# Context rows of a fused cross-attention issued from GpSimd's queue instead of SyncE's

## The reference, cut to what matters

```python
# x: (16, 64, 256), ctx_1024: (16, 1601, 256)
q = layernorm(x) @ Wq + bq
k = ctx_1024 @ Wk + bk
v = ctx_1024 @ Wv + bv
attn = softmax(einsum('bqd,bkd->bqk', q, k) / 16)
x = x + einsum('bqk,bkd->bqd', attn, v)
# then: selective-scan layer, ffn, windowed attention, masked attention, experts
```

## Time and profile before

| | us |
|---|---|
| median of 3 runs | 666.3 (665.47 to 666.42) |
| the profiled execution | 663.98 |
| its span (first to last instruction) | 662.2 |
| cross-attention, span 0 to about 158 | 158 |
| mean clock granted to TensorE, share of full | 0.994 |

### The profile page before, as it was taken

How to read it: one execution, slowest core, us unless ns; L and a number is a source line. 1 busy time by engine, 2 the same in 40 slices (tenths; PEclk the granted TensorE clock), 3 DMA queues, 4 the chain that set the end, 5 groups by cost and what they waited for, 6 DMA issues and landing times. The chain is left out here.

```text
span 662.2 us, 11724 instructions
## 1 busy us (share of the span) xinstructions
PE 603.9 (91%) x4436; PEld 461.4 (70%) x4436; DVE 465.1 (70%) x795; ACT 368.9 (56%) x700; POOL 235.2 (36%) x190
## 2 busy tenths in 40 slices
PE   8899999989998878878878999999999899999997
PEld 6555544455356767667767788887777767889897
DVE  2663333345867999999999527788978777886554
ACT  2411111124988999999999434334657466556343
POOL 2000000000069999999989200035651021231000
PEclk9899999999999999999999999999999989999999
DMA  8999999993922223232320000000100022210000
GB/s 306 402 402 394 388 393 392 389 334 143 269 75 97 97 97 97 96 127 97 125 97 4 1 1 17 1 0 19 36 2 2 1 65 81 64 49 1 32 1 33
DMA packets 31839, 86.48 MB, mean 131 GB/s; under 512 B 8108, under 2 KB 19848, under 8 KB 29608
## 3 DMA queue, kind: packets, MB, share of 16 engines
q1 hardware_dynamic: 31640, 85.67, 36.4%
q10 hardware_dynamic: 144, 0.06, 0.0%
HBM read 83.50 MB, written 1.11 MB: 128 GB/s over the span
## 5 line engine op out<-in xcount | busy, mean ns | idle before, releaser
L841 POOL TENSOR_TENSOR dbu<-du,bs 128x1024 f32<-128x1024 f32 x64 | 149.9, 2371 | 6.6 <-DVE w_in L1089 4.6
L970 ACT ACTIVATE weighed<-T,CT 128x256 f32<-128x256 f32 x222 | 95.0, 593 | 1.3 <-PE T L1168 0.9
L1089 DVE TENSOR_TENSOR_SCAN w_in<-hS,dbu 128x1024 f32<-128x1024 f32 x42 | 94.6, 2272 | 0.4 <-ACT hS L959 0.4
L959 ACT ACTIVATE hS<-delta,negA 128x504 f32<-128x504 f32 x128 | 90.9, 815 | 4.9 <-DVE xn L1089 2.2
L1182 PE MATMUL Y<-ident,weighed 128*128 128x128 f32 x512 | 66.7, 273 | 0.0
L1168 PE MATMUL T<-ident,w_in 128*128 128x128 f32 x336 | 46.0, 279 | 19.8 <-ACT weighed L970 14.3
L1182 PEld LDWEIGHTS Y<-ident,weighed 128*128 128x128 f32 x512 | 57.9, 141 | 0.5
L1168 PEld LDWEIGHTS T<-ident,w_in 128*128 128x128 f32 x336 | 36.1, 140 | 30.7 <-DVE w_in L1089 27.4
L309 PE MATMUL O<-cN,pT 128*64 128x256 f32 x384 | 46.7, 385 | 6.9 <-DMA cN<-in_ctx 6.9
L421 POOL COPY w_xp<-w_xp 128x64 f32<-128x64 f32 x3 | 0.6, 236 | 144.8 <-DMA w_out<-in_w_out 144.8
L1089 DVE TENSOR_TENSOR_SCAN xn<-hS,dbu 128x1024 f32<-128x1024 f32 x22 | 50.0, 2275 | 2.3 <-ACT hS L959 2.3
(11 more groups left out here) (442 smaller groups left out, 1338.4 us busy)
## 6 DMA issues: line engine op xcount, KB each, us to landing
cN<-in_ctx SPq DMA_DIRECT2D x8, 3072.0 KB, 25.7
cT<-in_ctxT SPq DMA_DIRECT2D x7, 3202.0 KB, 24.7
bs<-b_rows SPq DMA_DIRECT2D x32, 512.0 KB, 3.6
raw_w<-in_w SPq DMA_DIRECT2D x16, 256.0 KB, 2.8
cT<-in_ctxT SPq DMA_DIRECT2D x1, 2048.0 KB, 10.4
w<-in_w SPq DMA_DIRECT2D x7, 256.0 KB, 7.4
cT<-in_ctxT SPq DMA_DIRECT2D x1, 1154.0 KB, 13.5
vs<-vx SPq DMA_DIRECT2D x8, 136.0 KB, 2.3
```

What stands on the lines that cost most here:

```text
L841: e.tensor_tensor(dbu[s % NB][:, :, :], half(m.du, s // DS), row, ALU.mult).then_inc(s_bu, 1)
L959: i = e.activation(by_batch(A[s % 2][:, j * HALF:(j + 1) * HALF]), by_batch(m.delta[:, c, h * HALF:(h + 1) * HALF]), ACT.Exp, scale=m.negA ...
L970: i = e.activation(weighed[s % 2][:, q * Q:(q + 1) * Q], T[:, q * Q:(q + 1) * Q], ACT.Copy, scale=c_of(s, q))
L1089: e.tensor_tensor_scan(S[s % NS], A[s % 2][:, :], dbu[s % NB][:, :, :].rearrange("p c n -> p (c n)"), 0.0, ALU.mult, ALU.add).then_inc(s_h, 1)
```

## The change

GpSimd takes over the loads of the context rows and of the last rows, in a loop of its own behind the constants. Its first two tiles wait for nothing; tile i from 2 on waits for values(i-2), as before. SyncE keeps the tokens, the weights, the columns with their waits, and `loads`, which now follows the last columns directly. No computation is changed.

```diff
@@ block.sync
             first_loads(e)
-            load_rows(e, k, 0, 0)
-            load_rest(e, k, 0, 0)
             e.dma_start(k.wv0[:, :, :], k.w_v0.rearrange("(c p) n -> p c n", p=P)).then_inc(k.s_wv, 16)
-            for i in range(2, TILES + 1):
-                if i < TILES:
-                    e.wait_ge(s_sc, i - 1)
-                    load_columns(e, k, i, i % 2)
-                if i >= 3:
-                    e.wait_ge(s_pv, i - 2)
-                load_rows(e, k, i - 1, (i - 1) % 2)
-                load_rest(e, k, i - 1, (i - 1) % 2)
+            for i in range(2, TILES):
+                e.wait_ge(s_sc, i - 1)
+                load_columns(e, k, i, i % 2)
             loads(e)
@@ block.gpsimd
             constants(e)
+            for i in range(TILES):
+                if i >= 2:
+                    e.wait_ge(s_pv, i - 1)
+                load_rows(e, k, i, i % 2)
+                load_rest(e, k, i, i % 2)
             e.wait_ge(k.s_w2, k.n_w2)
```

## The result

| | before | after |
|---|---|---|
| median of the runs, us | 665.9 (664.0 to 666.4, 4 runs) | 675.8 (674.7 to 678.5, 4 runs) |
| the profiled execution, us | 663.98 | 675.12 |
| its span, us | 662.2 | 673.4 |
| mean clock granted to TensorE | 0.994 | 0.981 |

The changed kernel is slower. By the medians the difference is 9.9 us; the ratio on record is 1.0165 with an interval of 1.0135 to 1.0195, which is 11.0 us (9.0 to 13.0) of 665.9; the two profiled executions differ by 11.1. The forecast was +9.9 with bounds of +7.5 and +12, and all three figures lie within them, though the interval reaches a little beyond. Inside the trace the sum came together differently, and that is what the rest is about. One execution of a later experiment (one tile of rows) took 1002.3 us at a granted clock of 0.56, a slow state in which no other run was, and is left out of every figure.

What follows compares the result with a forecast made beforehand. TensorE's pace bounds the first cross-attention tiles, the DMA engines the later ones. Start 16.2, less waits 7.2, plus clock 0.9, gives +9.9 us: 673.9 for the profiled execution, 676.2 against the median; range 669 to 682.

Steps and rivals of the forecast that it cites:

- what the waits are worth: From scores(1) to values(7), TensorE's waits for loads come to 7.2 us, which early loads would give back.
- Turns by the packet: At the DMA engines, two full queues alternate packet by packet, not by bytes, and together are no faster than one.
- The start: Two tiles of rows pass SyncE's start loads; scores(1) move by +16.2 us, from 33.18 to 49.4.
- the loss of the tokens of tiles 1 to 3: At the start, these tokens land 16.2 us later, at about 30 instead of 13.7, as nearly all 48 row packets pass.
- The clock: TensorE idles about 10 us before the late tokens and then runs at a lower clock: +0.9 us, bounds 0 to 3.4.
- The lead: After the late start, loads are some 12 us ahead, shrinking 1.9 a tile, lasting the six tiles left; no load waits.
- The sum: At values(7), 16.2 - 7.2 + 0.9 = +9.9 us: 673.9 for the profiled execution, 676.2 against the median.
- The late weights: At the end, 2.8 MB (7.2 us) can pass ahead of the rows of tiles 6 and 7, covered by 4.6 us.
- The floor of 152.1: Latest landing of tile 7's rows; were the start free, values(7) would start then, +5.3 us.
- Sharing by bytes: At the start, SyncE's loads run at half speed instead of being overtaken; +5.3 us, 671.6, chance 0.16.
- a slower transfer: From 30 to 152, loads run at 345 GB/s instead of 389 and bind TensorE throughout; +16, 682 us, chance 0.13.
- no change: Rows get in only where SyncE's queue leaves room, or begin too late to alter the order; +0 to +1, 666.8, chance 0.08.

Runs made afterwards that it cites:

- new start alone: Against the changed kernel, GpSimd issues only rows 0 and 1, SyncE all others in the old order; 1.0112 of the kernel before, 7.4 us slower.
- one tile of rows: Against the changed kernel, GpSimd issues the rows of tile 1 only after scores(0); 1.0076 of the kernel before, 5.1 us slower.

## Why the prediction was right, step by step

**What bounds the kernel, and what the waits are worth.** Right. The old order makes the later tiles wait for 7.2 us; by the rows of before TensorE needs 89.08 us from scores(1) to scores(7) without them, and the kernel with the new start alone showed 89.07.

**Turns by the packet.** Right, and now shown: 203 against 205, 338 against 339 and, late in the stage, 201 against 205 packets. It was read from a quarter of a microsecond in which two small loads met.

**The start.** The mechanism was right, but one term was too large and the path was not followed to its end. Forecast was a shift of scores(1) by 16.2 us, plus 0.9 for the clock; measured were 14.2, with the clock in it.

The term is the loss of the tokens of tiles 1 to 3: 11.3 us, not 16.2. I had let nearly all 48 packets of the two tiles of rows pass on each engine before these tokens landed. The changed kernel's queues from 10 to 25, when they land:

```profile
q0 software_dynamic: 504, 5.15, 84.9%
q1 hardware_dynamic: 543, 0.87, 17.9%
```

504 packets of rows are 32 on each engine, two thirds of the 48, and two thirds of 16.9 us are the 11.3. A part of the error is the moment at which the rows begin to move. I had allowed 1 to 3 us from GpSimd's issue to its first packet; the windows 9.5 to 10.0 and 10.0 to 10.5 show the first packets of its queue about 4 us behind the issue at 5.84:

```profile
q0 software_dynamic: 3, 0.04, 17.9%
...
q0 software_dynamic: 13, 0.16, 76.1%
```

The larger part is the count of SyncE's packets that still stood before the tokens. I took all that move up to their landing, 902 from 9 and still 799, or 50 per engine, from 10. But by the trace's records of single packets 318 of these carry 2308 bytes, and so belong to the second part of the first columns, which was issued behind the tokens.

What stood behind the tokens lost the full time of two tiles, 16.5 us: the second part of the first columns (landing 33.3) and the tokens of tiles 4 to 7 (34.7). These became the later ones, and TensorE reached scores(1) from there. I had followed only the first loss, through the chain of work that was latest before. The timeline of the kernel before shows what that chain had to give:

```profile
17.38 2.17 PE L294 MATMUL S<-cT,qkT 128*64 128x512 f32 x16
...
24.95 0.76 PE L259 MATMUL O<-ident,prob 128*128 128x128 f32 x4 [2.58 <-DVE prob L544]
...
27.70 4.46 PE L270 MATMUL S<-xT,wq 128*128 128x256 f32 x16
```

The second half of scores(0) moved from 17.38 to 33.38, by 16.0 us. From it to scores(1) the kernel before took 15.8 us, with a wait of 2.6 us for VectorE and a stretch at the low clock; the changed kernel took 14.0. The wait is gone but for 0.1, and that, with the clock of the next paragraph, turns 16.0 into 14.2. So the 16.2 of the forecast came near the 16.0 of another load, and the slack of 2.5 us behind it was overlooked.

**The clock.** Put at 0.9 with bounds of 0 and 3.4. In the second half of scores(0) it costs 1.8 us. But the low clock that the kernel before had itself a little later is gone: the projection above takes 3.62 us instead of 4.46, and all steps of that stretch together 1.2 less. What the start pays is 0.6. Another 1.7 came at scores(7), where I had none.

**The lead.** This was the wrong step. The prediction had the waits for `cN` gone "and none for `cT` in their place", and waits for `cT` came. I had let the lead shrink by 1.9 us a tile for both kinds of loads. But with a packet of 12 KB against one of 6.4 KB the rows get two thirds of the bytes while both queues are full. The changed kernel's queues from 125 to 134:

```profile
q0 software_dynamic: 201, 2.47, 65.7%
q1 hardware_dynamic: 205, 1.24, 33.3%
```

The columns, issued by SyncE at nearly the same distance each time, took from issue to landing, for tiles 3, 4, 5, 6 and 7:

```profile
cT<-in_ctxT SPq DMA_DIRECT2D x1, 3202.0 KB, 11.6
...
cT<-in_ctxT SPq DMA_DIRECT2D x1, 3202.0 KB, 16.4
...
cT<-in_ctxT SPq DMA_DIRECT2D x1, 3202.0 KB, 20.5
...
cT<-in_ctxT SPq DMA_DIRECT2D x1, 3202.0 KB, 24.6
...
cT<-in_ctxT SPq DMA_DIRECT2D x1, 3202.0 KB, 26.9
```

The rows of tile 7 took only 14.3 us. So the columns took about 4 us longer from tile to tile up to tile 6, 2.3 at tile 7, and ran out at scores(7), while the rows had time to spare. I had used the packet rule at the start and forgotten it in the steady part. It cost 0.2 us at scores(6), 2.2 at scores(7) and the 1.7 of the clock behind it, 4.1 in all. The kernel with only the first two tiles of rows on GpSimd's queue has none of it.

**The sum.** Forecast 16.2 - 7.2 + 0.9 = 9.9. Measured at values(7) in the profiled executions: 14.2 - 7.2 + 4.1 = 11.1. The ratio gives 11.0, the medians 9.9. The mechanism held; the exact agreement with the medians is luck: a start put 2.9 too high with its clock, an end put 4.1 too low, and 1.2 of difference between the profiled executions and the medians.

**The late weights.** Right as far as could be told: covered. The floor of 152.1 never decided.

**The rivals.** Sharing by bytes and a slower transfer are excluded; from 60 to 120 the changed kernel moved 404 GB/s where before it was 387:

```profile
DMA packets 3143, 24.26 MB, mean 404 GB/s; under 512 B 249, under 2 KB 255, under 8 KB 2130
```

The rule of the Trainium skill that issuing from several engines saves only the time of issue ("DMA: Bandwidth & Descriptors", section "Issuing engines are not separate DMA queues") holds for the bandwidth of such a stretch to within 4%, but it would have given no change, and the tokens of tiles 4 to 7 arrived 16.5 us later. From 30 to 140, the stretch that the prediction named, it is 381 GB/s against 389, with some 6 us in it, from 50 to 56, in which the changed kernel had little to load.

## What to carry to other kernels

Where the DMA engines are the bound, a single queue in the order of need is a schedule, and a second queue takes it away: whatever is ready there passes what is needed. Before a load goes to another queue, count the packets of both queues that are ready at the same time, not the bytes. In these runs the one with the longer packets got more bytes, in their ratio. And look for such a case first at the start, where double buffers are both free and nothing holds the second queue back.

## What the runs showed of the hardware

While both are full, the queues of GpSimd and SyncE move the same number of packets: 203 to 205, 338 to 339, 201 to 205. GpSimd issued a tile of rows, three loads, in about 1.9 us of its own time, the largest of them in 0.75 to 0.93 us, against 0.37 for an unhindered one of SyncE. Its first packets moved about 4 us after the first issue, where I had expected 1 to 3. That is no constant: for the rows of tile 2 it was between 2.1 and 2.4 us (issue at 60.13, first packets between 62.25 and 62.50).

Also not expected: SyncE's load of the columns of tile 1 stayed 11.5 us in issue instead of 2.5. In the six profiles where GpSimd's rows move during the start it took 7.5 to 15.8 us, in the four others 2.5 to 3.3. That SyncE's queue was full while the other passed it would explain this; no run tested it.

```profile
6.92 11.48 SPq L85 DMA_DIRECT2D cT<-in_ctxT  x1
```
